# The sum of a weight slab's squares on TensorE: one bf16 product in place of two fp32 passes

## The chip, the cores and the metric

The kernel runs on one core of a Trainium2 chip. Its time is device microseconds of one execution, the median of several. Before the change it is 2371.62 us, the median of 3 runs (2368.73 to 2371.7). The profile was taken of a further execution of 2365.65 us, whose instructions span 2363.8 us. Engines are named as in the profile: PE (TensorE; PEld is its weight load), DVE (VectorE), ACT (ScalarE), POOL (GpSimd), SP (issues the DMAs).

## The reference

It is a stack of four pairs of cross attention and feed-forward block on x of 16 x 64 tokens x 512, each with a layernorm in front and a residual add behind. Cut to what the change touches:

```python
# attention of layer 0 (layers 2 and 3 are built alike, with other heads and a mask or a longer context)
q = (hidden_states @ q_proj_w.T).reshape(B, Q, 32, 128)      # 32 heads of 128
k = (cross_attention_states @ k_proj_w.T) ...                # 8 heads in layer 0
v = (cross_attention_states @ v_proj_w.T) ...
scores = einsum(q, k) * scale + mask
out = einsum(softmax(scores), v).reshape(B, Q, 32 * 128)
return out @ o_proj_w.T
```

The reference has no sum of a weight's squares. The kernel needs it for its own number format: it multiplies in fp16, each fp32 operand split into a high and a low half, and scales each slab of weights by a power of the slab's own sum of squares so that the halves fit fp16. The results are divided by the same scale again. So the sum need not be exact: the scale and its inverse are made from one number.

## The kernel before

The program is one sequence of blocks: `Setup`, attention 0, a feed-forward block, a narrow attention (layer 1), a feed-forward block, attention 2, a feed-forward block, attention 3, the last feed-forward block. Each engine has its own instruction list, written out by hand in `Attention.events`, and engines meet at semaphores only.

An attention block (class `Attention`, layers 0, 2 and 3) goes over 8 groups of 4 heads, and over 8 token tiles for each group: 64 units in 8 slots a period. In a slot PE makes, in the order of `events`: the scores of unit b, perhaps a sum of squares (`w_sum`), a projection tile, the transposes of the probabilities (line 611), perhaps another tile, the product with the values (`mix`), and the product with the output weights (`out`). Every product of halves is three fp16 matmuls, lines 84, 85 and 86 (`mm3`). Layer 0 also normalises q and k: line 580 sums the squares of q over the partitions, 32 matmuls of one bf16 column.

The weights come slab by slab (o, q, k, v of the next group) by DMA into `raw`, 128 x 2048 or 128 x 512 fp32. A slab takes these steps:

1. ACT squares it and adds the squares along each partition into one column of `w_ss` (line 309, `squares`; the slab's elements go to a scratch place).
2. PE adds the 128 partial sums over the partitions, with a 128 x 128 matrix of ones as the stationary operand, into one column of PSUM bank 7 (line 481, `sum_squares`). This is what the change edits.
3. DVE copies the total to `w_tot` (line 674), POOL makes the scale and the inverse from it (lines 890 and 893).
4. ACT makes the high half (line 314), DVE the low half (line 680).

Layer 0 and layer 2 have 3 slabs ahead of the block, 28 inside and 1 more (32), layer 3 has 18: 82 sums in all. The sums ahead of a block are issued from the block before it (`sum_ahead`, called at lines 1582, 1810, 1954 and 1965). Inside the block `w_sum` comes right behind the scores of its slot. The scores matmuls in front of it have 128 moving columns in layer 2, 64 in layer 0.

What the order depends on: the lists themselves. PE runs its list in order and waits at line 481 for the squares (`w_ss`) and for bank 7 to be read (`misc_read`).

Of the kernel before, what the change touches and what calls it, by code (L numbers as in the profile page):

```python
# [8 lines left out]
BF16 = mybir.dt.bfloat16  # L9
# [83 lines left out]
class Attention:  # L93
# [383 lines left out]
    def sum_squares(self, pe, j, ss_count, free):  # L477
        k, s = self.k, self.s
        pe.wait_ge(*s["misc_read"].by(free))
        pe.wait_ge(*s["w_ss"].by(ss_count))  # L480
        pe.matmul(k.bank[7][:, 0:1], k.ones[:, :], k.w_ss[:, j % 2:j % 2 + 1],
                  start=True, stop=True).then_inc(s["misc"].sem, 1)

    def sum_ahead(self, pe, j):
# [1798 lines left out]
```

## Time and profile before

| | |
|---|---|
| time, median of 3 | 2371.62 us (2368.73 to 2371.7) |
| the profiled execution | 2365.65 us, span 2363.8 us |
| PE busy | 2200.5 us, 93% |
| DVE, ACT, POOL busy | 1334.5, 1137.0, 540.9 us |
| granted TensorE clock, mean | 0.972 |
| fp32 passes of line 481 | 164, for 82 sums |

How to read it: PE's busy time is a union of modelled intervals. Matmuls are pipelined, and a row's duration (0.38 us for 512 columns, say) is longer than the time that it takes from PE, which is the distance from its start to the start of the next. So what a matmul costs is read from starts. Line 481 is one `matmul` in the code and two matmul records (and two weight loads) in the trace, since its operands are fp32. The blocks lie in the span at about these times: attention 0 from 45 to 600 us, attention 2 from 870 to 1600 us, attention 3 from 1730 to 2300 us.

### The profile page before, as it was taken

The page shows a single profiled execution, that of the slowest core. Times are in us where ns is not written, and L with a number is a line of the kernel's source. Part 1 is how long each engine was busy: PE and PEld are TensorE (multiplying, and loading weights), DVE is VectorE, ACT ScalarE, POOL GpSimd, SP SyncE. Part 2 cuts the span into 40 slices and gives each one's busy share as a digit, 9 for nine tenths or more (in the row PEclk, how much of TensorE's full clock was granted, in tenths as well). Part 3 has the DMA queues.
Part 4 walks back from the last instruction along what each step waited for, and adds up shares of the span by engine and source line. Part 5 has one row for each costly group of instructions (what it writes and reads, how often), then busy time and mean ns, then how long its engine had stood idle before and what let it go on. Part 6 is the DMA issues. An engine that isn't in the chain of part 4 may idle for free.

```text
span 2363.8 us, 40920 instructions
## 1 busy us (share of the span) xinstructions
PE 2200.5 (93%) x14366; PEld 1246.1 (53%) x14366; DVE 1334.5 (56%) x2695; ACT 1137.0 (48%) x2988; POOL 540.9 (23%) x936
## 2 busy tenths in 40 slices
PE   4889899999999889999999999998879899999998
PEld 2555555656644444555555555555434455555564
DVE  5566666666752465555555655555542455555554
ACT  4556565656412245555554555533322466556551
POOL 3332323233220322222212222212210122222221
PEclk9899999999989999999999999999979999999999
DMA  3110101100021011111111111101210111111010
GB/s 121 46 46 23 47 23 47 42 28 19 25 107 47 37 58 66 63 48 65 49 59 54 46 65 48 48 12 41 90 36 1 36 37 37 37 38 47 7 32 36
DMA packets 27384, 107.22 MB, mean 45 GB/s; under 512 B 4074, under 2 KB 12522, under 8 KB 17186
## 3 DMA queue, kind: packets, MB, share of 16 engines
q1 hardware_dynamic: 26722, 104.36, 12.5%
q8 instruction: 131, 2.15, 0.4%
q14 instruction: 83, 0.68, 0.1%
q10 hardware_dynamic: 448, 0.03, 0.0%
HBM read 102.29 MB, written 2.10 MB: 44 GB/s over the span
## 4 chain that ended last, share of the span: by engine, by line
PE 63%; DVE 15%; ACT 12%; issue 8%; POOL 1%; DMA 0%; ACTq 0%; DVEq 0%; POOLq 0%
PE bank L84 17%; PE bank L85 17%; PE bank L86 17%; ACT m_E L427 3%; PE bank L1786 3%; PE bank L1432 2%; PE bank L611 2%; DVE m_Sm L835 2%; DVE m_x L881 2%; DVE m_A L875 2%; ACT m_arena L309 1%; PE bank L1332 1%; ACT m_arena L409 1%; DVE m_arena L680 1%; DVE m_nmax L852 1%
## 5 line engine op out<-in xcount | busy, mean ns | idle before, releaser
L781 DVE TENSOR_TENSOR m_arena<-bank,m_arena 128x512 f16<-128x512 f32 x320 | 220.8, 690 | 509.9 <-ACT m_arena L409 509.5
L84 PE MATMUL bank<-m_input_parts,m_arena 128*128 128x512 f16 x1088 | 416.8, 383 | 8.0 <-DVE m_arena L781 2.3
L85 PE MATMUL bank<-m_input_parts,m_arena 128*128 128x512 f16 x1088 | 416.5, 383 | 0.0
L86 PE MATMUL bank<-m_input_parts,m_arena 128*128 128x512 f16 x1088 | 416.3, 383 | 0.0
L427 ACT ACTIVATE m_E<-m_Sm,m_nmax 128x64 f32<-128x64 f32 (+1 forms) x512 | 185.4, 363 | 422.5 <-DVE m_nmax L852 237.2
L893 POOL TENSOR_TENSOR m_E<-m_E,m_rinv 128x512 f32<-128x512 f32 (+1 forms) x192 | 177.5, 925 | 866.9 <-DVE m_rinv L866 866.9
L409 ACT ACTIVATE m_arena<-bank 128x512 f16<-128x512 f32 x320 | 189.6, 593 | 235.8 <-PE bank L86 235.4
L84 PE MATMUL bank<-m_wo_t,m_A 128*128 128x512 f16 x768 | 295.8, 385 | 0.0
L85 PE MATMUL bank<-m_wo_t,m_A 128*128 128x512 f16 x768 | 294.8, 384 | 0.0
L86 PE MATMUL bank<-m_wo_t,m_A 128*128 128x512 f16 x768 | 293.4, 382 | 0.0
L423 ACT ACTIVATE m_E<-bank,m_nmax,m_qk 128x128 f32<-128x128 f32 x256 | 113.7, 454 | 184.7 <-DVE m_nmax L823 184.7
L84 PE MATMUL bank<-m_arena,m_input_parts 128*128 128x128 f16 (+1 forms) x768 | 187.7, 275 | 1.7 <-DVE m_arena L781 0.9
L86 PE MATMUL bank<-m_arena,m_input_parts 128*128 128x128 f16 (+1 forms) x768 | 187.7, 275 | 0.0
L85 PE MATMUL bank<-m_arena,m_input_parts 128*128 128x128 f16 (+1 forms) x768 | 187.7, 275 | 0.0
L890 POOL TENSOR_TENSOR m_w_scale<-m_w_tot,m_consts 128x1 f32<-128x1 f32 x82 | 44.8, 546 | 589.4 <-DVE m_w_tot L674 556.8
L86 PEld LDWEIGHTS bank<-m_input_parts,m_arena 128*128 128x128 f16 x1088 | 107.3, 99 | 131.3 <-issue 5.1
L881 DVE SCALAR_TENSOR_TENSOR m_x<-bank,m_osc,m_x 128x512 f32<-128x512 f32 x192 | 143.0, 745 | 52.3 <-PE bank L86 52.3
L84 PEld LDWEIGHTS bank<-m_input_parts,m_arena 128*128 128x128 f16 x1088 | 110.9, 102 | 116.2 <-issue 6.1
L85 PEld LDWEIGHTS bank<-m_input_parts,m_arena 128*128 128x128 f16 x1088 | 107.2, 99 | 105.7 <-issue 4.5
L870 DVE TENSOR_TENSOR m_PT<-bank,m_PT 128x512 f16<-128x512 f32 (+1 forms) x192 | 112.1, 584 | 69.7 <-ACT m_PT L435 68.5
L611 PE MATMUL bank<-m_ident,m_E 128*128 128x128 f32 x640 | 104.3, 278 | 47.4 <-POOL m_E L893 47.3
L875 DVE TENSOR_TENSOR m_A<-bank,m_A 128x512 f16<-128x512 f32 x192 | 131.0, 682 | 0.2
(278 smaller groups left out, 4387.6 us busy)
## 6 DMA issues: line engine op xcount, KB each, us to landing
m_raw<-a_q SPq DMA_DIRECT2D x24, 1024.0 KB, 4.9
m_raw<-a_o SPq DMA_DIRECT2D x24, 1024.0 KB, 4.9
m_raw<-a_k SPq DMA_DIRECT2D x9, 1024.0 KB, 5.5
m_raw<-a_v SPq DMA_DIRECT2D x9, 1024.0 KB, 5.0
m_bias_in<-bias SPq DMA_DIRECT2D x64, 128.0 KB, 2.0
m_arena<-f_w SPq DMA_DIRECT2D x3, 1024.0 KB, 7.3
m_x<-x SPq DMA_DIRECT2D x2, 1024.0 KB, 7.1
m_arena<-ctx_t SPq DMA_DIRECT2D x4, 512.0 KB, 12.3
```

What stands on the lines that cost most here:

```text
L84: pe.matmul(out, lhs[0], rhs[0], start=first, stop=False)
L85: pe.matmul(out, lhs[0], rhs[1], start=False, stop=False)
L86: return pe.matmul(out, lhs[1], rhs[0], start=False, stop=last)
L409: act.activation(self.dest(name, part, 0), self.shaped(name, src), ACT.Copy).then_inc(s["proj_hi"].sem, 1)
L423: ins = act.activation(k.E[:, b % 2, cols], bank[2 + b % 2][:, cols], ACT.Exp, bias=k.nmax2[:, b % 2, h:h + 1], scale=qk, accum_out=k.rsum ...
L427: ins = act.activation(k.E[:, b % 2, cols], k.Sm[:, b % 2, cols], ACT.Exp, bias=k.nmax[:, b % 2, h:h + 1], accum_out=k.rsum[:, b % 2, h:h ...
L611: ins = pe.transpose(bank[4][:, j * P:(j + 1) * P], k.E[:, b % 2, j * P:(j + 1) * P], k.ident[:, :])
L781: ins = dve.tensor_tensor(self.dest(name, part, 1), self.shaped(name, bank[m % 2][:, :]), self.dest(name, part, 0), ALU.subtract)
L870: dve.tensor_tensor(self.pt_dst(b, 1), bank[4][:, 0:self.keys * HG], self.pt_dst(b, 0), ALU.subtract).then_inc(s["turned_lo"].sem, 1)
L875: dve.tensor_tensor(self.mix_dst(b, 1), self.mix_src(), self.mix_dst(b, 0), ALU.subtract).then_inc(s["mixed_lo"].sem, 1)
L881: dve.scalar_tensor_tensor(out=k.x[:, pair, :], in0=bank[6][:, :], scalar=k.osc[:, g:g + 1], in1=k.x[:, pair, :], op0=ALU.mult, op1=ALU.ad ...
L893: pool.tensor_tensor(out, a, b, op).then_inc(sem.sem, 1)
```

## The change

One operand pair of one matmul is changed. The stationary operand is now `ones_b`, the 128 x 128 matrix of ones in bf16, which the kernel already has (line 2060) and uses at lines 580 and 1960. The moving operand is the upper two bytes of each fp32 partial sum, read as bf16: its value cut to 8 significant bits.

```diff
@@ sum_squares
         pe.wait_ge(*s["misc_read"].by(free))
         pe.wait_ge(*s["w_ss"].by(ss_count))
-        pe.matmul(k.bank[7][:, 0:1], k.ones[:, :], k.w_ss[:, j % 2:j % 2 + 1],
+        pe.matmul(k.bank[7][:, 0:1], k.ones_b[:, :], k.w_ss[:, j % 2:j % 2 + 1].bitcast(BF16)[:, 1:2],
                   start=True, stop=True).then_inc(s["misc"].sem, 1)
```

No instruction moves on any engine: each list has the same rows in the same order, and the same waits and semaphore increments. At each of its places the matmul of line 481 reads other operands, and what was two records becomes one.

## Rows read from the trace of the kernel before

**Rows 1.** The page: busy time of the engines; the chain of waits by engine.
```profile
PE 2200.5 (93%) x14366; PEld 1246.1 (53%) x14366; DVE 1334.5 (56%) x2695; ACT 1137.0 (48%) x2988; POOL 540.9 (23%) x936
...
PE 63%; DVE 15%; ACT 12%; issue 8%; POOL 1%; DMA 0%; ACTq 0%; DVEq 0%; POOLq 0%
```

**Rows 2.** By stage: us; busy of PE, PEld, DVE, ACT, POOL; clock; DMA share; GB/s.
```profile
114.00:568.00 454.00, 419.21 (x3766) 263.04 (x3763) 290.79 (x677) 270.28 (x833) 138.57 (x235) 0.95 0.11 36
905.00:1545.00 640.00, 637.83 (x4014) 344.09 (x4015) 377.02 (x683) 325.10 (x765) 135.43 (x246) 1.00 0.16 54
1870.00:2260.00 390.00, 383.93 (x2542) 224.75 (x2541) 225.19 (x413) 232.60 (x646) 83.20 (x146) 1.00 0.09 31
```

**Rows 3.** The chain of waits by line, shares of the stretch from 930 to 1545 us.
```profile
by line: PE bank L84 32.0%; PE bank L85 31.9%; PE bank L86 31.9%; PE bank L611 3.6%; PE bank L481 0.7%; issue 0.0%
```

**Rows 4.** Line 481 from 905 to 1545 us, then from 1870 to 2260 us.
```profile
L481 PE MATMUL bank<-m_w_ss,m_ones x54: 222/236/250, 909.5 to 1541.1; 128*128 128x1 f32 x54
...
L481 PE MATMUL bank<-m_w_ss,m_ones x26: 222/250/272, 1887.1 to 2230.5; 128*128 128x1 f32 x26
```

**Rows 5.** Timeline of PE in attention 2 around a sum: start, us, line, tiles.
```profile
977.99 0.22 PE L85 MATMUL bank<-m_arena 128*128 128x128 f16 x1
978.05 0.22 PE L86 MATMUL bank<-m_arena 128*128 128x128 f16 x1
978.10 0.33 PE L481 MATMUL bank<-m_w_ss,m_ones 128*128 128x1 f32 x2
978.30 0.38 PE L84 MATMUL bank<-m_arena,m_input_parts 128*128 128x512 f16 x1
...
1002.57 0.33 PE L481 MATMUL bank<-m_w_ss,m_ones 128*128 128x1 f32 x2
```

**Rows 6.** Timeline of PE in attention 0: one-column bf16 matmuls of line 580, and behind.
```profile
318.96 0.95 PE L580 MATMUL bank<-m_ones_b,m_arena 128*128 128x1 bf16 x32
319.77 0.19 PE L84 MATMUL bank<-m_arena 128*128 128x64 f16 x1
```

**Rows 7.** Timeline of PE at the start of attention 2.
```profile
873.93 0.38 PE L86 MATMUL bank<-m_input_parts,m_arena 128*128 128x512 f16 x1
874.15 0.28 PE L481 MATMUL bank<-m_w_ss,m_ones 128*128 128x1 f32 x2
874.29 0.38 PE L84 MATMUL bank<-m_input_parts,m_arena 128*128 128x512 f16 x1
```

**Rows 8.** Timeline of PE in attention 3, then PE's waits from 1870 to 2260 us.
```profile
1853.14 0.35 PE L481 MATMUL bank<-m_w_ss,m_ones 128*128 128x1 f32 x2 [2.73 <-ACT m_arena L309]
1853.35 0.38 PE L84 MATMUL bank<-m_input_parts,m_arena 128*128 128x512 f16 x1
...
1959.41 0.38 PE L481 MATMUL bank<-m_w_ss,m_ones 128*128 128x1 f32 x2 [0.63 <-ACT m_arena L309]
1959.65 0.38 PE L84 MATMUL bank<-m_input_parts,m_arena 128*128 128x512 f16 x1
...
PE bank L481 <- ACT m_arena L309: 4.4, 6, 1.2
```

**Rows 9.** Pieces of the chain of waits: start, us, what.
```profile
19.70 0.56 PE bank L481 x2
...
264.65 0.38 PE bank L481 x2
...
1951.20 0.05 DVE m_x L881
```

**Rows 10.** PE's waits from 114 to 568 us: us in total, times, longest.
```profile
PE bank L611 <- POOL m_E L893: 31.1, 12, 2.6
```

**Rows 11.** Two stretches of attention 0, columns as in rows 2.
```profile
322.90:325.60 2.70, 0.10 (x3) 0.07 (x2) 2.67 (x7) 0.00 (x0) 2.43 (x4) 1.00 0.00 0
325.70:329.10 3.40, 3.40 (x15) 2.24 (x15) 1.29 (x5) 2.41 (x10) 2.94 (x2) 0.50 0.23 77
329.10:340.50 11.40, 11.40 (x78) 5.94 (x77) 6.76 (x17) 7.66 (x21) 1.22 (x2) 1.00 0.01 2
```

## The prediction

> **What bounds the kernel now.** I read the page first: PE is busy 93% of the span, and the chain of waits runs over PE for only 63% of it [rows 1]. So a shorter PE list is worth its full price in some stages and little in others, and the stages have to be taken apart.
>
> The busy time by stage does that [rows 2]. From 905 to 1545 us (attention 2) PE is busy 637.8 of 640 us, at the full clock (1.00, 2.4 GHz). From 1870 to 2260 us (attention 3) it is busy 383.9 of 390. From 114 to 568 us (attention 0) it is busy 419.2 of 454, at a mean clock of 0.95. The chain by line says the same of attention 2: lines 84, 85, 86 and 611, all PE, and 0.7% of line 481, with nothing of another engine [rows 3]. There every nanosecond off PE's list is one off the time. 0.7% of 615 us is 4.3 us, for the 25 sums of that stretch: 0.17 us each.
>
> In attention 0 PE waits 12 times for POOL's normalised probabilities, 31.1 us in all and up to 2.6 us each [rows 10]; one sits at 322.9 to 325.6 us [rows 11]. In front of that wait PE arrives early. The chain there is a ping-pong of ACT (exponentials, conversions) and DVE (softmax, low halves), and PE is on it only at the loop's heads, as at 264.65 us [rows 9].
>
> **What the change removes and adds.** The two fp32 passes of a sum become one bf16 pass of one column. No instruction is moved, no wait is added, no DMA changes, and DVE reads the same fp32 total behind it. All that counts is how long PE is held.
>
> Before: in attention 2 the last scores matmul starts at 978.05 and the projection tile behind the sum at 978.30, 0.252 us by the trace's unrounded starts [rows 5]. The scores matmul itself takes the distance of its kind, 977.99 to 978.05, some 0.056 us. The sum thus holds PE for 0.196 us, as if two weight loads of an fp32 operand lay one behind the other, with one moving column to hide them.
>
> After: the trace has the very kind of matmul that comes: one moving column, bf16, a full 128 x 128 stationary operand, with fp16 matmuls behind. It is line 580. 32 of them start at 318.96, and the fp16 matmul behind at 319.77, so 0.81 us for 32, 0.025 us each [rows 6]. There `ones_b` is the moving operand and here the stationary one; both are bf16 of the same shape. I take 0.025 us. The bounds for the new pass: below, nothing is cheaper in the trace than that; above, one of the two fp32 passes, 0.11 us: PE goes on 0.21 to 0.24 us behind the start of a pair [rows 8].
>
> The saving for a sum by its place:
>
> - Attention 2, behind scores of 128 columns: 0.252 - 0.081 = 0.171 us. 54 records from 905 to 1545 us are 27 sums [rows 4], none with a wait. 27 x 0.171 = 4.6 us.
> - Attention 2, first period, two sums behind 512-column matmuls: 873.93 to 874.29 is 0.356 us, and would be 0.216 + 0.025 = 0.241. The longer matmul in front hides one weight load already [rows 7]. 2 x 0.115 = 0.2 us.
> - Attention 3: 26 records are 13 sums [rows 4]. The first (1887.1) is in a stretch where DVE and ACT lead: nothing. Six stand in the stream as in attention 2: 6 x 0.171 = 1.0 us. Six wait for ACT's squares, 4.4 us in all, and PE goes on 0.24 us behind the start of the sum [rows 8]; that becomes 0.03. 6 x 0.21 = 1.3 us. The squares that they wait for hang, through ACT's and DVE's lists, on an output product that PE made 8 us before, so what PE gains ahead of it isn't eaten by this wait: the chain of waits has DVE's residual add of that product at 1951.20 [rows 9].
> - Single ones on the chain: at 1853.14, and alike at 1843 and 829 us, PE resumes 0.21 us behind the start, which becomes 0.03: 3 x 0.18 = 0.5 us [rows 8]. At 264.65 [rows 9] and once more at 415 us 0.21 each, 0.4 us. At 52.6 us, 0.2. At 19.70, and alike at 41.6, early in the program, a sum is a piece of 0.56 us, of which about 0.35 stays: 0.4 us for both [rows 9].
> - The other 33 sums, 27 of them in attention 0, are off the chain. What hides them there is the wait for POOL: there are two sums for each of the 12 waits [rows 10], so PE comes 0.4 us earlier and waits 0.4 us longer. If that cover weren't there, 33 x 0.2 = 6.6 us more would be saved, not lost.
>
> Sum: 4.6 + 0.2 + 1.0 + 1.3 + 0.5 + 0.4 + 0.2 + 0.4 = 8.6 us. From the profiled execution's 2365.65 us this gives 2357.0. That execution was 6.0 us below the median of the runs shown, 2371.62, and I forecast for the median: 2371.6 - 8.6 = 2363.0 us. With 0.11 us for the new pass the 49 sums on the chain save 0.085 less each, 4.2 us less: 2367.2.
>
> The trace and the Trainium skill differ on what an fp32 product is: "FP8 and Floating Point Precision", TensorE Precision Notes, has true fp32 as 4 passes through the array. This trace has 2 records a sum [rows 4], and the 0.196 us is measured for them together, so the sum goes by the trace. By 4 passes of 0.1 us the saving would be about twice as large, some 17 us; no row here shows it.
>
> **The rivals.**
>
> *The new pass isn't cheap.* A switch from fp16 to bf16 and back, or a load of `ones_b` that is slower than line 580's, could hold PE for as long as one fp32 pass. Against it stands that line 84 follows line 580 at the same 0.025 us [rows 6]. It would give 2367.2 us by the sum above; with a little noise this can't be told from no change.
>
> *All of it counts.* If the ping-pong in attention 0 leans on PE more than the chain says (a tile finished just when ACT wants it), its 27 sums pay too: 8.6 + 6.6 = 15.2 us, 2356.4. Against it: PE is idle there for 31 us [rows 10].
>
> *The gain is taken back in attention 2 or 3.* DVE (377.0 of 640 us) and ACT (325.1) have room [rows 2], and PE never waits, so nothing is near. If attention 2 (4.8 us) and attention 3 (2.3) give back all, 8.6 - 7.1 = 1.5 us stay: 2370.1.
>
> *Slower: the clock in attention 0.* This is one mechanism. Each long wait for POOL is followed by a stretch at half the clock: 2.6 us idle, then a granted clock of 0.50 (1.2 GHz) from 325.7 to 329.1, then 2.4 GHz again [rows 11]. The change makes each of these waits 0.4 us longer. If a longer wait brings a second such stretch of 3.4 us, PE does 1.7 us less work behind it. With 12 waits [rows 10] that is up to 20 us, against 8.6 gained: 2371.6 + 11.8 = 2383.4. It decides from 0.72 us lost per wait (8.6 / 12). For it: such a stretch follows the wait already. Against: a second stretch would have to begin when PE is busy again without a gap, and the busy half-clock stretch (3.40 us busy of 3.40) ended in the full clock [rows 11]. The Trainium skill has a rule for it, in "TensorE: Matmul & The Clock Gate", section Why this matters for your kernels: no long idle gaps between bursts, since the clock falls to half behind one. By that rule, the trace agrees: half the clock came behind a gap of 2.6 us.
>
> **How the numbers follow.** My forecast (a pass of about 0.025 us, attention 0 pays next to nothing) has 0.70; its own range is 2360 to 2366. The dear pass has 0.08, all of it 0.08, the gain taken back 0.08, the clock 0.06. About 0.2% (4.7 us) is what a measurement can tell from no change. The forecast and the case where all counts are faster, 0.78; I take off 0.03 for a median that lies a few us off, as the profiled execution does. Faster 0.75. Of the rest the dear pass and the gain taken back are no change, with what was taken off: 0.19. Slower 0.06. The range of 2355 to 2370.5 holds all cases but the clock, whose chance and a little noise are what it leaves out.
>
> **What would show it.** In the profile after, line 481 has 82 records, not 164. In attention 2 the distance from the last scores matmul to the projection tile is 0.08 us, not 0.25; at 0.16 the pass is dear. The distance from sum to sum in attention 2, 24.47 us before (978.10 to 1002.57) [rows 5], shrinks to about 24.30. In attention 0 the distance from sum to sum at the same place of two groups stays as it is, and PE's 12 waits grow to some 3 us each; if the group gets shorter by 0.4 us, all of it counts. If the granted clock from 114 to 568 us is under 0.95, and the groups are longer, it was the clock. The forecast is wrong if attention 2 doesn't get shorter by 4 to 5 us.

## Result, and the profile after

The changed kernel takes 2360.71 us, the median of 6 runs (2359.42 to 2363.18), against 2371.34 us (6 runs, 2368.73 to 2372.11) before: ratio 0.9958, 95% interval 0.9948 to 0.9968. That is 10.6 us less by the medians and 10.0 by the ratio (7.6 to 12.3). The forecast was 2363.0 us, 8.6 less than the median then known. A second measurement (below) gave 0.9955.

The page of the changed kernel, the lines that answer to [rows 1]:

```profile
PE 2179.8 (92%) x14284; PEld 1224.4 (52%) x14284; DVE 1335.0 (57%) x2695; ACT 1138.0 (48%) x2988; POOL 541.1 (23%) x936
...
PE 65%; DVE 14%; ACT 11%; issue 7%; POOL 1%; DMA 0%; ACTq 0%; DVEq 0%; POOLq 0%
```

PE has 82 matmul records and 82 weight loads fewer, one of each for every sum, and no other engine changed its count. All records of line 481, of the whole run:

```profile
L481 PEld LDWEIGHTS bank<-m_w_ss,m_ones_b x82: 95/98/152, 19.6 to 2225.5; 128*128 128x128 bf16 x82
L481 PE MATMUL bank<-m_w_ss,m_ones_b x82: 163/167/211, 19.6 to 2225.6; 128*128 128x1 bf16 x82
```

The timeline of PE in attention 2, the place of [rows 5]:

```profile
981.19 0.22 PE L86 MATMUL bank<-m_arena 128*128 128x128 f16 x1
981.25 0.17 PE L481 MATMUL bank<-m_w_ss,m_ones_b 128*128 128x1 bf16 x1
981.27 0.38 PE L84 MATMUL bank<-m_arena,m_input_parts 128*128 128x512 f16 x1
```

From 981.19 to 981.27 it is 0.084 us by unrounded starts, before 0.252. The new pass holds PE for 0.028 us (forecast 0.025), and the sum's saving is 0.168 us.

Busy time by stage, the stretches and columns of [rows 2]:

```profile
114.00:568.00 454.00, 406.98 (x3737) 251.60 (x3736) 291.85 (x681) 269.30 (x830) 138.47 (x234) 0.99 0.11 36
905.00:1545.00 640.00, 637.28 (x4006) 341.00 (x4005) 379.02 (x688) 327.75 (x776) 136.22 (x248) 1.00 0.17 55
1870.00:2260.00 390.00, 384.76 (x2538) 223.82 (x2537) 226.66 (x415) 233.84 (x648) 83.67 (x146) 1.00 0.09 30
```

In attention 2 PE is as busy as before, and DVE, ACT and POOL each do a little more in the same 640 us (DVE 379.0 us, before 377.0): the stage runs faster as a whole. In attention 0 PE's busy time fell by 12 us and the others' rose by some 1 us at most: PE waits more. Most of that is the clock and not the sums (0.95 before, 0.99 here): a kernel below (fp32 twice in layer 2), with the old sums in attention 0 and 6.8 us of the stage at half the clock where before had 41.0, has PE busy for 409.4 us. PE's waits from 114 to 568 us, to be held against [rows 10]:

```profile
PE bank L611 <- POOL m_E L893: 31.2, 12, 2.6
PE bank L580 <- DVE m_w_tot L674: 10.0, 12, 0.9
PE bank L84 <- DVE m_arena L786: 3.9, 11, 0.4
```

The wait for the probabilities is what it was. Longer are the waits at line 580 (before 2.9 us, 4 times) and at line 84 behind a sum (before 0.3 us, twice). Those at line 580 go with the clock: that same kernel has 9.6 us there, 12 times. At line 84 it has 1.6 us, so of the 3.9 us some 2 can be the time that the sums gave.

To see where the time went I cut each kernel's span at the same VectorE instructions, the first ones of the kernel before behind the times in the header. Us of each stage, from one profiled execution each:

| kernel | 0 to 112.5 | to 568 | to 640 | to 720 | to 905 | to 1545 | to 1840 | to 1900 | to 2260 | span |
|---|---|---|---|---|---|---|---|---|---|---|
| before | 112.72 | 455.71 | 72.48 | 80.11 | 184.49 | 640.46 | 295.20 | 59.48 | 361.31 | 2363.8 |
| before, again | 112.39 | 455.98 | 72.52 | 79.92 | 184.48 | 640.25 | 295.18 | 59.50 | 361.47 | 2363.6 |
| changed | 111.46 | 455.50 | 74.03 | 84.12 | 184.05 | 635.97 | 293.61 | 59.12 | 359.11 | 2358.9 |
| changed, again | 111.70 | 455.75 | 74.02 | 81.36 | 184.22 | 635.88 | 293.27 | 59.10 | 359.05 | 2356.2 |

Behind 2260 us each has another 101.9 us.

The two profiled executions of before lie 5 us below the median of its timed runs. Their stages from 568 to 720 us are 1.5 and 1.3 to 4.2 us shorter than the changed kernel's, and code and work are the same there. So what the spans show is too little by about that; the stages that the change touches are what is compared below. The stage from 1545 to 1840 us is 1.7 us shorter in the changed kernel, but this can't be put down to the sums: in the nine other kernels below it takes from 293.0 to 298.2 us, in no order with their sums.

### The profile page after: what moved, and what is told of

Same layout as the page of the kernel before. It is cut to its first block, busy times and chain, and to the rows that moved or that the text cites. A ratio compares the mean times of both kernels' runs of the same rounds, so it can differ in the third digit from the quotient of the medians.

```text
span 2358.9 us, 40756 instructions
## 1 busy us (share of the span) xinstructions
PE 2179.8 (92%) x14284; PEld 1224.4 (52%) x14284; DVE 1335.0 (57%) x2695; ACT 1138.0 (48%) x2988; POOL 541.1 (23%) x936
## 4 chain that ended last, share of the span: by engine, by line
PE 65%; DVE 14%; ACT 11%; issue 7%; POOL 1%; DMA 0%; ACTq 0%; DVEq 0%; POOLq 0%
PE bank L84 18%; PE bank L85 17%; PE bank L86 17%; PE bank L1786 3%; ACT m_E L427 2%; PE bank L1432 2%; PE bank L611 2%; DVE m_Sm L835 2%; DVE m_x L881 2%; ACT m_arena L309 2%; ACT m_arena L409 1%; DVE m_A L875 1%; PE bank L1332 1%; DVE m_arena L680 1%; DVE m_nmax L852 1%
## 6 DMA issues: line engine op xcount, KB each, us to landing
m_arena<-ctx_t SPq DMA_DIRECT2D x4, 512.0 KB, 12.3
```

## The experiments

Each was timed beside the kernel before, on the same chip.

**The parts alone.** In `sum_squares`, with L = 0, 2 or 3:

```diff
+        if self.layer == L:
+            pe.matmul(k.bank[7][:, 0:1], k.ones_b[:, :], k.w_ss[...].bitcast(BF16)[:, 1:2], ...)
+        else:
             pe.matmul(k.bank[7][:, 0:1], k.ones[:, :], k.w_ss[...], ...)
```

> The bf16 pass in attention 0 and the sums ahead of it alone (32 sums); the other 50 stay in two fp32 passes. Theory (the chain of waits decides; PE has slack in attention 0): 5 sums on the chain give 1 to 1.3 us, ratio 0.9995, not to be told from no change. Rival (all sums count): 32 x 0.2 = 6.4 us, ratio 0.9973. In the trace of the changed kernel the half-clock stretches in attention 0 became fewer; if these are what brought time there, this kernel is faster by more than 1.3 us.

> The bf16 pass in attention 2 and the sums ahead of it alone (32 sums). Theory: 27 x 0.168 + 2 x 0.112 + 0.18 = 5.0 us, ratio 0.9979; the distance from sum to sum 24.30 us. Rival (the gain is made elsewhere, and attention 2 gives its part back): under 2 us.

> The bf16 pass in attention 3 and the sums ahead of it alone (18 sums). Theory: 6 x 0.168 + 6 x 0.16 to 0.21 + 2 x 0.18 = 2.4 to 2.7 us, ratio 0.9989. If the three parts (layers 0, 2, 3) add to about 8.7 us, the 10.6 us measured of the whole change are that and scatter; if they add to about 10.6, one of the prices was too low, and the part that is over its sum says which.

Measured: layer 0 alone 0.9995 (0.9986 to 1.0004), 1.2 us; layer 2 alone 0.9971 (0.9960 to 0.9983), 6.9 us; layer 3 alone 0.9989 (0.9980 to 0.9998), 2.6 us. That attention 0 pays fully (0.9973) is out. By these ratios the parts add to 10.7 us, and the whole gave 10.0 and 10.7 in its two measurements. But layer 2 alone is over its 5.0 us, and its trace says why. Stages again:

| kernel | 905 to 1545 | 1900 to 2260 |
|---|---|---|
| layer 0 alone | 640.65 | 359.85 |
| layer 2 alone | 636.26 | 359.86 |
| layer 3 alone | 640.78 | 359.11 |

Attention 2 gives 4.2 us, as the sums say. And attention 3 is 1.5 us shorter than before in the two kernels that left its sums in fp32. What it lost there is seen in two views. First the queue of instruction fetches from 1970 to 2240 us: packets, MB, share. Before:

```profile
q8 instruction: 21, 0.34, 0.5%
```

Layer 2 alone, and the changed kernel, each read:

```profile
q8 instruction: 3, 0.05, 0.1%
```

Then PE's waits from 1970 to 2240 us in the kernel before:

```profile
PE bank L481 <- ACT m_arena L309: 2.5, 4, 0.6
PE bank L84 <- issue: 1.0, 2, 0.5
```

PE's code for attention 3 is a loop of two groups that runs three times; its branches stand at 1990.7, 2105.2 and 2219.7 us. Just behind the first two, at 1993.97 and 2108.47 us, PE waited for nothing that the profile shows ("issue"). In the kernel before the queue brings 9 packets between each two branches, by the packets' start times; in the changed kernel none starts between 1976.7 and 2220.6 us. In the changed kernel and in the three parts these waits are gone. Of the 13 profiled executions of this document the six with 20 or 21 packets have such waits, and the seven with 2 or 3 have none. So I take them as waits for instructions that had not arrived. Each part alone already saves these 1.5 us. The parts should then add to some 3 us more than the whole, which their intervals, 2 to 3 us either way for each, can't show.

How many instructions the change took out of PE's code is less than the records say, since a loop's code stands there once and runs three times. The code has 42 sums: 16 each for layers 0 and 2, and 10 for layer 3. The change took 42 matmuls and 42 weight loads out of it, 74 of these 84 ahead of attention 3's loop. Layer 0 alone and layer 2 alone took out 32 each, all ahead of the loop.

**More passes in place of fewer.** Before, with the fp32 product written twice in layer 0, or in layer 2; and the changed kernel with the bf16 product written twice everywhere:

```diff
+        if self.layer == 0:      # or 2
+            pe.matmul(k.bank[7][:, 0:1], k.ones[:, :], k.w_ss[...], start=True, stop=True)
         pe.matmul(k.bank[7][:, 0:1], k.ones[:, :], k.w_ss[...], start=True, stop=True).then_inc(...)
```

> The kernel before, with each sum of attention 0 (32) made twice in fp32, the first result overwritten by the second: four passes in place of two, 0.22 us more of PE for each. Theory (PE has slack in attention 0): the 5 sums on the chain give 1.1 us, and the rest is hidden: ratio 1.0005. Rival (PE leads there as much as ACT and DVE): 32 x 0.22 = 7 us, ratio 1.0030.

> The kernel before, with each sum of attention 2 (32) made twice in fp32: four passes in place of two. Theory (every nanosecond of PE's list counts there): 30 x 0.22 = 6.6 us, ratio 1.0028, the distance from sum to sum 24.69 us. Rival (the sum's price by its starts is too low or too high, as the 8.2 us of the kernel with the bf16 pass in attention 2 alone would have it): 9 us or more, or under 4.

> The changed kernel with the bf16 pass made twice for each of the 82 sums, the first overwritten by the second. Theory: a further pass holds PE for 0.028 us, so attention 2 gets 27 x 0.028 = 0.8 us longer, distance from sum to sum 24.33 us, and the whole about 1.2 us over the changed kernel: ratio to the kernel before about 0.9963. Rival (what a bf16 pass costs is a switch between fp16 and bf16, paid once for both): no difference, 24.30 us. Rival (a second load of the same weights can't be hidden): 0.1 us each, 24.40 us.

| kernel | ratio (95%) | 0 to 112.5 | to 568 | 905 to 1545 | 1900 to 2260 |
|---|---|---|---|---|---|
| fp32 twice, layer 0 | 1.0010 (1.0001 to 1.0019) | 112.34 | 455.42 | 640.81 | 363.51 |
| fp32 twice, layer 2 | 1.0033 (1.0020 to 1.0045) | 111.86 | 455.45 | 646.40 | 364.78 |
| bf16 twice | 0.9976 (0.9967 to 0.9986) | 110.89 | 455.44 | 636.67 | 361.44 |

The stage from 112.5 to 568 us took 25 sums of twice the length and didn't get longer: its slack is shown from the other side. Of the 2.4 us of that kernel 2.1 stand in attention 3, which it didn't touch (363.5 against 361.4). Attention 2 got 5.9 us longer by 27 x 0.22 us, as PE's list there counts in full; another 3.4 us stand in attention 3 (the whole is 7.8 us longer by its ratio). A second bf16 pass costs attention 2 0.7 us: the distance from scores to tile grew from 0.084 to 0.109 us, 27 x 0.025. So nearly all of the first one's 0.028 us is the pass and not a switch of formats. But the kernel is 4.3 us over the changed one by the two ratios, not 1.2: PE's code is as long as before, the 21 packets are back, and so are the waits for issue from 1970 to 2240 us:

```profile
PE bank L84 <- issue: 1.6, 2, 0.9
```

**The length of the list alone.** The changed kernel, with 82 one-column products at the start of PE's list. They stand outside any loop, so they add 164 instructions to its code. The expectation below takes the list to be as long as before. That holds for the instructions that run; as code it is 80 instructions longer.

```diff
         pe.wait_ge(*s["fill"].by(1))
+        for _ in range(82):
+            pe.matmul(k.bank[7][:, 0:1], k.ones_b[:, :], k.ones_b[:, 0:1], start=True, stop=True)
         pe.wait_ge(*s["wq"].by(1))
```

> The changed kernel with 82 one-column bf16 products put into PE's list at the very start, where PE is idle (until 10 us) for the first real product; they write bank 7, which nobody reads then. So PE's list is as long as in the kernel before, and the sums are the cheap ones. Theory (part of the gain is code: with the list shortened, PE's loop in attention 3 no longer fetches instructions again, 21 packets of 16 KB before from 1970 to 2240 us and 3 after; the fetch makes PE late at two loop heads): the 21 packets and PE's waits for issue come back, attention 3 (from 1900 to 2260 us of the kernel before) takes 361.3 us or more and not 359.1, and the whole is 1.5 to 2.5 us over the changed kernel, ratio to before 0.9965 to 0.9970. Rival (the fetches depend on the loop's own length, which the padding leaves as in the changed kernel): 3 packets, 359.1 us, ratio 0.9957.

It measured 1.0015 (1.0006 to 1.0024), some 14 us over the changed kernel, so the direction was right and the size far too small. The start got no longer (111.82 us to the first mark). The sums are the cheap ones and stand 24.30 us apart in attention 2, which takes 637.80 us, with two longer distances of 25.29 and 25.22 us at loop heads. Attention 3 takes 367.88 us in place of 359.1. The two stages hold 10.7 of the 14 us. The instruction fetches and PE's waits from 1970 to 2240 us:

```profile
q8 instruction: 20, 0.33, 0.5%
```

```profile
PE bank L84 <- issue: 6.3, 4, 2.6
PE bank L481 <- ACT m_arena L309: 2.7, 4, 0.8
```

Products that ran 1900 us earlier, in PE's idle time, made attention 3 nearly 9 us longer. The rival (the loop's own length decides) is out: the loop is the changed kernel's, and layer 0 alone has the old loop without the fetches. What goes with the stage is the code ahead of the loop. PE's matmuls and weight loads in it, counted from the code against the kernel before (the loop itself has 8 fewer where attention 3's sums are in one bf16 pass):

| kernel | ahead of the loop | packets, 1970 to 2240 | waits for issue | 1900 to 2260 |
|---|---|---|---|---|
| changed, twice | -74 | 3, 3 | 0, 0 | 359.1, 359.1 |
| later sum in attention 3 (below), two ways | -74 | 2, 2 | 0, 0 | 369.5, 359.3 |
| layer 0 alone, layer 2 alone | -32 | 2, 3 | 0, 0 | 359.9, 359.9 |
| layer 3 alone | -10 | 2 | 0 | 359.1 |
| before, twice | 0 | 21, 21 | 1.0, 1.1 | 361.3, 361.5 |
| bf16 twice | 0 | 21 | 1.6 | 361.4 |
| fp32 twice, layer 0, layer 2 | +64 | 20, 20 | 2.9, 4.1 | 363.5, 364.8 |
| padded | +90 | 20 | 6.3 | 367.9 |

Between 10 instructions fewer and none the fetches set in, and above that the waits grow with the code. (The 369.5 us have another cause, told below.) But more code ahead of the loop also moves the loop to another place in memory, and no run here moves it without changing the number of instructions. So whether the number or the place decides stays open.

**Null and second look.**

> The kernel before, unchanged, once more, for a second profile and a null comparison. Theory (the first profile of it, 5.5 us below the median of its timed runs, caught a short passage of the stage from 640 to 720 us, with 13.7 us at half the clock): ratio 1.000, and a profile near 2371 us that is 3 to 4 us longer in that stage, with some 24 us at half the clock. Rival (its stages are as in the first profile, and the difference lies in the stages that the change shortens): the stage from 640 to 720 us is as long as before, and attention 2 or 3 is longer than 631.5 us from first to last sum of its 27.

> The changed kernel once more, beside the padded one and on its chip, for a second profile and a second ratio. Theory (8.6 us of sums as forecast, less what attention 3 did not give, and 2 us of code): ratio 0.9957 to 0.9963, attention 2's sums 24.30 us apart, 2 or 3 instruction packets from 1970 to 2240 us. Rival (the first ratio, 0.9958, was scatter, and 8.6 us or less is right): 0.9965 or above.

Before again: 0.9999 (0.9990 to 1.0008). Its profiled execution (2365.77 us) is once more the lowest of its 11 runs, with the short stages (80 us from 640 to 720); the other ten take 2369.7 to 2372.8. So my guess that a second profile would catch the long passage failed; what differs in the timed runs of before has no trace. The changed kernel again: 0.9955 (0.9942 to 0.9969), attention 2 and 3 as in the first profile.

**A later sum in attention 3.** PE waits there for ACT's squares, 4.8 us in all (from 1870 to 2260 us of the changed kernel):

```profile
PE bank L481 <- ACT m_arena L309: 4.8, 6, 1.4
```

Two kernels take the wait away: `w_sum` behind the slot's tile; and the second sum one slot later, with its conversion:

```diff
-            if made is not None:
+            if made is not None and self.layer != 3:
                 out.append(("w_sum", made, misc))
...
             if todo:
                 out.append(("tile", todo.pop(0), slot // 4))
+            if made is not None and self.layer == 3:
+                out.append(("w_sum", made, misc))
+                misc += 1
```

```diff
                 made = slot // 2 if slot % 2 else None
+                if self.layer == 3:
+                    made = {1: 0, 4: 1}.get(slot)
```

> The changed kernel, and in attention 3 the event w_sum stands behind the slot's projection tile, no longer ahead of it, on PE, DVE and POOL alike. In the changed kernel PE waits there 6 times for the squares, 4.8 us in all. Theory (PE leads in attention 3 and each of its idle stretches is worth its length): the waits go, and the time is 4 to 4.8 us below the changed kernel, about 14 us below the kernel before, ratio 0.9940. Rival (the scale comes 2.6 us later to POOL, ACT and DVE, and the halves of the slab come late, or another wait takes the place): same as the changed kernel, ratio 0.9958, or above.

> The changed kernel, and in attention 3 the second slab's sum, scale and conversion (q) stand one slot later, in slot 4 and not 3, at the same place within the slot; the squares stay in slot 2. Theory (the waits of 0.64 to 1.4 us for the squares, 4.8 us in all, are PE's only idle time there, and the order of POOL within the slot is kept): 3 to 4.5 us below the changed kernel, ratio to before about 0.9942. Rival (PE is early there, since ACT and DVE are late from the first slab's conversion; without this wait it waits at the next place, for the probabilities or a tile's low half): no difference to the changed kernel, 0.9958.

The first measured 0.9993 (0.9984 to 1.0002), 8 us over the changed kernel. The wait is gone and three others stand in its place (from 1895 to 2255 us; its lines are numbered 3 higher):

```profile
PE bank L84 <- DVE m_arena L784: 7.6, 6, 1.3
PE bank L614 <- POOL m_E L896: 2.7, 12, 0.3
PE bank L614 <- DVE m_PT L873: 2.3, 6, 0.9
```

The second measured 0.9951 (0.9937 to 0.9965), the same as the changed kernel beside it (0.9955). Its waits from 1895 to 2270 us (its lines are numbered 2 higher):

```profile
PE bank L84 <- DVE m_arena L783: 5.9, 6, 1.0
```

It is the rival's outcome. PE is early at that place and waits for ACT or DVE, at line 481 or, without that wait, at the next line 84. That the first slab's conversion is what makes them late was not tested. No version that beats the changed kernel was found.

## Why the prediction was right, and where not

By stages, from the profiles of kernels that have the stage as before and as changed:

| term | forecast | measured |
|---|---|---|
| attention 2, 27 sums | 4.6 | 4.4 (640.36 to 635.93, means of two) |
| the two behind 512 columns, and 829 us | 0.4 | 0.3 (184.48 to 184.14; a place behind 512 columns takes 0.244 us, before 0.356) |
| attention 3, 12 sums in the loop | 2.3 | 0.8 (359.85 to 359.08) |
| 1843 and 1853 us | 0.4 | 0.4 (59.49 to 59.11) |
| start, to 112.5 us | 0.6 | 1.0 (112.56 to 111.58), but five executions with the old sums there lie from 111.86 to 112.72 |
| attention 0, loop heads | 0.4 | 0.2 (455.85 to 455.63), not to be told from none: the same five lie from 454.82 to 455.98 |
| attention 3, instruction fetches | not seen | 1.5 (361.39 to 359.86) |

They add to 8.6 us, the forecast's total, and that is in part luck: 1.5 us that attention 3 kept back were made up by 1.5 us of fetches that no term had. The interval of the whole begins at 7.6. The 1 to 2 us that are missing to its 10.0 or 10.6 are not placed: the stage from 1545 to 1840 us has 1.7, which are not shown to be the change's, and the timed runs of before have no trace.

- **The new pass.** Right. It holds PE for 0.028 us, so line 580 was the right row to take, and neither the dear pass (0.11) nor a switch of formats exists.
- **Attention 2.** Right: the mechanism and the size, shown by taking a pass away (4.4 us) and by adding two (5.9 us). The distance from sum to sum is 24.30 us as forecast.
- **Attention 0.** Right that it pays next to nothing: doubled sums there cost it nothing. Wrong in where the slack would appear. I had the 12 waits for POOL grow to 3 us; they stayed at 2.6. What the sums gave is seen behind the second sum of a group, where PE waits for DVE's low half.
- **Attention 3.** The failed step: "so what PE gains ahead of it isn't eaten by this wait". It is. In the changed kernel the wait in every second group is 0.77 us where it was 0.64, and a group lasts 56.72 to 56.83 us where it took 56.86 to 56.92 in the kernel with layer 0 alone. So a group gives some 0.13 us (0.8 us in all over six groups), not 0.38. I also had PE go on 0.03 us behind a sum that waited. It takes 0.08:

```profile
1956.47 0.18 PE L481 MATMUL bank<-m_w_ss,m_ones_b 128*128 128x1 bf16 x1 [0.64 <-ACT m_arena L309]
1956.55 0.39 PE L84 MATMUL bank<-m_input_parts,m_arena 128*128 128x512 f16 x1
```

  Against [rows 8] it saves 0.16 us behind the wait, not 0.21. And that too is taken back at once: the next scores matmul, which reads DVE's low half, starts 6.56 us behind the sum (1956.47 to 1963.03), as it does in the kernel with layer 0 alone (1964.13 to 1970.69). The later sums fit this: without the wait at line 481 PE waits for DVE at line 84. ACT and DVE bound that part of the group. That PE was busy 383.9 of 390 us didn't say so.
- **What made up for it.** The 1.5 us of instruction fetches were in no term. [rows 3] could not show them, as they are in attention 3. A trace of before does, in PE's waits for issue at two loop heads and in the packets of the instruction queue.
- **The clock rival.** Out. Attention 0 had 41.0 and 37.5 us at half the clock in the two traces of before, and 10.2 and 23.9 in those of the changed kernel, with the same wait of 2.6 us in front. That the change brought this about is not shown: three kernels with the old sums there had 13.7, 23.9 and 6.8 us. The stage took 455.7 and 456.0, and 455.5 and 455.75 us, and 455.45 us in the one with 6.8. So in this stage, where PE isn't on the chain, some 30 us at half the clock cost under 1 us.

## What to carry to other kernels

A small product on the bounding engine is priced by the distance from the start of the matmul in front to the start of the one behind, with another matmul of the coming kind as the price after; it counts in full only where the engine never waits. In a stage with even one wait a group, ask of that wait whether its chain holds the saving; here it held two thirds, and the engine's 98% busy time didn't tell. And an edit that changes the length of an engine's code should be read with the instruction queue beside it (32 instructions were enough here): count them in the code, where a loop stands once, take one part alone, and look at the stages that it doesn't touch.

## What the runs showed of the hardware

- A one-column bf16 product with a 128 x 128 stationary operand holds PE for 0.028 us in a stream of fp16 products and for 0.08 us behind a wait; the fp32 form, two passes, for 0.196 and 0.24 us.
- Instructions added in front of everything, run while PE was idle, made a loop 1900 us later 8.8 us longer. With the packets of the instruction queue at 2 or 3 in 270 us PE had no wait for issue there; with 20 or 21 these waits were 1.0 to 6.3 us. In 13 profiled executions no count was between 3 and 20. The high ones came with the code ahead of the loop as long as before or longer, the low ones with it 10 to 74 instructions shorter; number or place is open.
